# Cross-attention stage of a one-core perceiver block: scores as three fp32r products, exponentials kept in the banks of the scores

## The reference

```python
q_hk = (hidden_q @ Wq.T).reshape(Bv, Sv, H, K)            # 64 batches, 32 queries, 16 heads, K = 128
q_big = rope(jnp.einsum('bshk,hkq->bshq', q_hk, w_kc_q))
kv_r = _apply_rope(kv_c, sin_k[None], cos_k[None])         # (64, 257, 128)
q_r = jnp.einsum('bshq,hqr->bhsr', q_big, W_qr)
k_r = jnp.einsum('bld,hdr->bhlr', kv_r, W_kr)
scores = jnp.einsum('bhsr,bhlr->bhsl', q_r, k_r)
attn = jax.nn.softmax(scores, axis=-1)
ctx_c = jnp.einsum('bhsl,bld->bhsd', attn, kv_r)
ctx_lat = jnp.einsum('bhsd,hkd->bhsk', ctx_c, w_kc_kv)
return ctx_lat.transpose(0, 2, 1, 3).reshape(Bv, Sv, H * K) @ Wo.T
```

## Time and profile before

| | us |
|---|---|
| median of 3 runs | 1603.71 (1599.01 to 1604.7) |
| the profiled execution | 1602.14, its span 1600.3 |
| busy in the span | PE 1482.6, DVE 1151.1, ACT 810.9, POOL 514.5 |
| cross-attention stage | from 460 to about 960 |
| granted PE clock, mean | 0.972 |

### The profile page before, as it was taken

One profiled execution on the slowest core, in us unless ns is written; L12 is line 12 of the kernel. 1 busy time (PEld: TensorE's weight loads), 2 busy tenths in 40 slices (PEclk: granted clock), 3 DMA queues, 4 the chain that ended last, 5 costly groups with the idle time before them and its releaser, 6 DMA issues. The chain is left out here.

```text
span 1600.3 us, 26575 instructions
## 1 busy us (share of the span) xinstructions
PE 1482.6 (93%) x8136; PEld 1122.0 (70%) x8136; DVE 1151.1 (72%) x2076; ACT 810.9 (51%) x1739; POOL 514.5 (32%) x466
## 2 busy tenths in 40 slices
PE   5799999999967999999999977999898899999997
PEld 3577777777746778777787756888443478787876
DVE  6888777887649888888888753767687735656466
ACT  4566566656545555555555433555211355554554
POOL 4244333542024444444444313221351202222021
PEclk9899999999999999999999988999898899999999
DMA  4223334243575555555555514000244100000000
GB/s 153 70 83 107 105 110 125 73 123 90 187 210 117 114 120 111 131 108 125 112 121 115 127 20 172 0 0 0 84 175 159 43 1 1 27 1 26 0 27 27
DMA packets 140918, 140.06 MB, mean 88 GB/s; under 512 B 84150, under 2 KB 111926, under 8 KB 139708
## 3 DMA queue, kind: packets, MB, share of 16 engines
q1 hardware_dynamic: 140284, 138.54, 32.5%
q10 hardware_dynamic: 576, 0.81, 0.2%
HBM read 109.88 MB, written 27.39 MB: 86 GB/s over the span
## 5 line engine op out<-in xcount | busy, mean ns | idle before, releaser
L1002 ACT ACTIVATE c_e<-c_sc_ps,c_peak 128x257 f32<-128x257 f32 x256 | 119.6, 472 | 215.3 <-DVE c_peak L895 215.3
L874 POOL TENSOR_TENSOR c_mixed_low<-c_whole,c_mixed_high 128x512 fp32r<-128x512 f32 x64 | 81.6, 1275 | 256.8 <-ACT c_mixed_high L1022 256.8
L77 DVE TENSOR_TENSOR b_rot_parts_low<-b_rot,b_rot_parts_high 128x1536 fp32r<-128x1536 f32 x64 | 136.5, 2132 | 21.9 <-ACT b_rot_parts_high L541 21.9
L1578 PE MATMUL f_ps<-f_right,f_left 128*128 128x512 f32 x256 | 115.5, 613 | 8.7 <-ACT f_raw L1621 6.3
L278 POOL TENSOR_TENSOR b_turned_raw<-b_turn_part 128x384 f32<-128x384 f32 x32 | 70.0, 2189 | 164.4 <-DVE b_key_parts_low L77 163.2
L895 DVE TENSOR_REDUCE c_peak<-c_sc_ps 128x2 f32<-128x514 f32 x128 | 88.5, 691 | 44.9 <-PE c_sc_ps L1068 43.4
L70 PE MATMUL c_out_ps<-c_shared_high,c_mixed_high 128*128 128x512 f32 x256 | 112.4, 439 | 8.5 <-issue 8.5
L324 DVE TENSOR_TENSOR b_rot<-b_w_qr,b_angle 128x1536 f32<-128x1536 f32 x64 | 118.6, 1852 | 0.2
L70 PE MATMUL b_ps<-c_shared_high,b_wq_parts_high 128*128 128x512 f32 x256 | 108.4, 423 | 6.5 <-DVE c_shared_low L77 6.5
L70 PE MATMUL e_mm_ps<-folded_high,e_h_t_high 128*128 128x512 f32 x256 | 106.4, 416 | 5.7 <-DVE e_h_t_low L77 5.6
L541 ACT ACTIVATE b_rot_parts_high<-b_rot 128x1536 fp32r<-128x1536 f32 x64 | 95.2, 1488 | 24.5 <-PE b_ps L72 17.0
(11 more groups left out here) (232 smaller groups left out, 3937.2 us busy)
## 6 DMA issues: line engine op xcount, KB each, us to landing
c_ends_spread<-end_weights SPq DMA_DIRECT2D x64, 256.0 KB, 3.8
carried_queries<-x SPq DMA_DIRECT2D x7, 2048.0 KB, 11.3
b_early<-early SPq DMA_DIRECT2D x15, 640.0 KB, 4.0
f_left<-ent_in SPq DMA_DIRECT2D x16, 512.0 KB, 5.2
f_right<-ent_out SPq DMA_DIRECT2D x16, 512.0 KB, 6.5
c_q_first<-carried_queries SPq DMA_DIRECT2D x32, 224.0 KB, 3.3
c_q<-carried_queries SPq DMA_DIRECT2D x32, 224.0 KB, 3.4
b_late<-late SPq DMA_DIRECT2D x16, 320.0 KB, 3.8
```

The lines of the kernel that those rows point to most:

```text
L77: return nc.vector.tensor_tensor(low, value, high.bitcast(F32), ALU.subtract)
L874: nc.gpsimd.tensor_tensor(mixed[1][:, w, :, u], whole[:, u % 2].rearrange("p (h s) -> p h s", h=H), mixed[0][:, w, :, u].bitcast(F32), ALU ...
L1002: last = nc.scalar.activation(e[:, v, c], sc_ps[:, 2 * v + c, 0:L], ACT.Exp, bias=peak[:, v, c:c + 1], accum_out=total[:, v, c:c + 1])
L1578: return nc.tensor.matmul(ps[:, m], left[:, slot, m * P:(m + 1) * P], right[:, slot], start=k == 0, stop=k == CF - 1)
```

## The change

The queries and the rotated keys are split into high and low parts (`round_queries`, `round_keys` on ACT, `split_queries`, `split_keys` on POOL), and the scores become three fp32r products each, over 258 columns with one column of zeros. The exponentials are written over the scores in PSUM. One DVE instruction takes them from there, times the inverse sums, into `e` of 2x256; the 257th is taken by a product of its own from PSUM. So the banks are free only when both have read them. To make room, raw keys have two buffers instead of four, the rotation works in `spare`, and so the load of the next stage's weights waits for the last rotation. The last two heads of batches 0 and 1 come by DMA out of `staged`. The diff, cut:

```diff
@@ query_path, SP, last
             crossing.output_weights(sp, w_vo_dram, 2)
+            sp.wait_ge(qc_stored, 8 * HPAIRS)
+            crossing.staged_queries(sp, staged)
@@ query_path, ACT
-                    if isinstance(U, int) and U >= 2 * HPAIRS - 2:
-                        at = (H - 2 + ab) * S + base
-                        nc.scalar.activation(crossing.q[:, :, at:at + G], ...)
@@ Crossing
+    def staged_queries(self, sp, staged):
+        for u in range(2):
+            sp.dma_start(self.q[:, u, (H - 2) * S:].bitcast(F32), staged[:, u].rearrange("p h s -> p (h s)")).then_inc(self.q_loaded[u], 16)
@@ cross_attention, SP
                     if known(i, 1):
                         store_ends(i - 1, u)
-                        wait(sp, rotated_, b - BT + 1)
-                        crossing.load(sp, b, u)
+                    wait(sp, rotated_, b - 1)
+                    crossing.load(sp, b, u % 2)
+                    if known(i, 1):
                         spread_ends(i - 1, u)
-            for u in range(2, BT):
-                crossing.load(sp, u, u)
             in_tiles(sp, tile)
+            sp.wait_ge(rotated_, B)
             holo.load(sp, holo_loaded)
@@ cross_attention, POOL
+            def split_queries(b, u):
+                pool.wait_ge(q_rounded, b + 1)
+                nc.gpsimd.tensor_tensor(q[u], q[u].bitcast(F32), q_high[:, u % 2].bitcast(F32), ALU.subtract).then_inc(q_split, 1)
+            def split_keys(b, u):
+                pool.wait_ge(key_rounded, b + 1)
+                nc.gpsimd.tensor_tensor(keys[1][:, u % 2], kv_even[u], keys[0][:, u % 2].bitcast(F32), ALU.subtract).then_inc(key_split, 1)
             def tile(i, w):
                 for j in range(STEPS):
+                    if half == 0 and not (isinstance(b, int) and (b == 0 or b + 1 >= B)):
+                        split_keys(b + 1, (u + 1) % BT)
                     if half == 0 and not (isinstance(b, int) and b + 2 >= B):
                         rotate(b + 2, (u + 2) % BT, i + (u + 2) // BT)
+                    if half == 1 and not (isinstance(b, int) and b + 2 >= B):
+                        split_queries(b + 2, (u + 2) % BT)
                     if half == 1 and (u or known(i, 1)):
                         split_mixed(b - 1, (u - 1) % BT, w if u else 1 - w)
@@ cross_attention, DVE
-                for c in range(2):
-                    last = nc.vector.tensor_scalar(e[:, v, c], e[:, v, c], inverse[:, v, c:c + 1], None, ALU.mult)
-                last.then_inc(normed, 1)
+                wait(dve, turned, n - 1)
+                nc.vector.tensor_tensor(e[:, v], sc_ps[:, 2 * v:2 * v + 2, 0:END], inverse[:, v].unsqueeze(2).to_broadcast([P, 2, END]),
+                                        ALU.mult).then_inc(normed, 1)
-                dve.wait_ge(normed, n + 1)
-                nc.vector.tensor_copy(ends[:, v, 2 * half:2 * half + 2], e[:, half, :, END]).then_inc(ended, 1)
+                nc.vector.tensor_tensor(ends[:, v, 2 * half:2 * half + 2], sc_ps[:, 2 * half:2 * half + 2, END], inverse[:, half],
+                                        ALU.mult).then_inc(ended, 1)
-            parts = [two pieces of the angles, in crossing.q and q_later]
+            parts = [three pieces, in raw_pair, swapped_pair and table]
@@ cross_attention, ACT
             def exponential(n, v):
                 act.wait_ge(peaked, n + 1)
-                wait(act, turned, n - 1)
-                wait(act, ended, n - 1)
-                    last = nc.scalar.activation(e[:, v, c], sc_ps[:, 2 * v + c, 0:L], ACT.Exp, ...)
+                    last = nc.scalar.activation(sc_ps[:, 2 * v + c, 0:L], sc_ps[:, 2 * v + c, 0:L], ACT.Exp, ...)
+                    if not (isinstance(b, int) and b + 2 >= B):
+                        if half == 0:
+                            round_queries(b + 2, (u + 2) % BT, i + (u + 2) // BT)
+                        else:
+                            round_keys(b + 2, (u + 2) % BT)
@@ cross_attention, PE
                 if half == 0:
-                    pe.wait_ge(q_loaded[u], queries_in(u, t))
-                    pe.wait_ge(rotated_, b + 1)
-                wait(pe, exped, n - 1)
+                    pe.wait_ge(q_split, b + 1)
+                    pe.wait_ge(key_split, b + 1)
+                wait(pe, normed, n - 1)
+                wait(pe, ended, n - 1)
-                    last = nc.tensor.matmul(sc_ps[:, 2 * half + c, 0:L], q[u][:, at], kv_t[u], start=True, stop=True)
+                    last = multiply_parts(nc, sc_ps[:, 2 * half + c, 0:LE], [q_high[:, u % 2, at], q[u][:, at]], [a[:, u % 2] for a in keys], True, True)
```

More of the change, by code:

```diff
@@ L730, in rotate_first @@
         nc.gpsimd.tensor_tensor(part[:, 1], self.swapped[0], self.table[:, 1], ALU.mult).then_inc(self.pool_chained, 1)
+        nc.gpsimd.memset(self.keys[:, L:], 0.0).then_inc(self.padded, 1)
         pool.wait_ge(self.pool_chained, 2)
-        nc.gpsimd.tensor_tensor(self.keys[:], part[:, 0], part[:, 1], ALU.add).then_inc(self.rotated, 1)
+        pool.wait_ge(self.padded, 1)
+        nc.gpsimd.tensor_tensor(self.keys[:, 0:L], part[:, 0], part[:, 1], ALU.add).then_inc(self.rotated, 1)
     def first(self, sp):
@@ L752, in cross_attention @@
         END = L - 1
-        raw_later, swapped_later = sb("c_raw_later", [P, BT - 2, L]), sb("c_swapped_later", [P, BT - 2, L])
-        crossing.raw += [raw_later[:, u] for u in range(BT - 2)]
-        crossing.swapped += [swapped_later[:, u] for u in range(BT - 2)]
         table, raw, swapped = crossing.table, crossing.raw, crossing.swapped
         table_loaded, raw_loaded = crossing.table_loaded, crossing.raw_loaded
-        part = sb("c_part", [P, 2, L])
-        kv_later = sb("c_kv_t", [P, BT - 1, L])
-        kv_t = [crossing.keys[:]] + [kv_later[:, u] for u in range(BT - 1)]
+        part = spare[:, 0:2 * L].rearrange("p (n l) -> p n l", n=2)
+        LE = L + 1
+        kv_later = sb("c_kv_t", [P, BT - 1, LE])
+        kv_even = [crossing.keys[:]] + [kv_later[:, u] for u in range(BT - 1)]
+        kv_t = [a[:, 0:L] for a in kv_even]
         kv = pair("c_kv", [P, BT, 2, P])
-        q_later = sb("c_q", [P, BT - 2, H * S])
+        q_later = sb("c_q", [P, BT - 2, H * S], F32R)
         q = [crossing.q[:, u] for u in range(2)] + [q_later[:, u] for u in range(BT - 2)]
+        q_high = sb("c_q_high", [P, 2, H * S], F32R)
+        keys = pair("c_key", [P, 2, LE])
         peak = sb("c_peak", [P, 2, 2])
@@ L798, in queries_in @@
         def queries_in(u, t):
-            return 32 * t + (16 if u < 2 else 32)
+            return 32 * (t + 1)
         def in_tiles(engine, tile):
@@ L1016, in round_kv, with round_queries, round_keys @@
                 nc.scalar.activation(kv[0][:, u], kv_ps[:, 0:2 * P].rearrange("p (k x) -> p k x", k=2), ACT.Copy).then_inc(kv_rounded, 1)
+            def round_queries(b, u, t):
+                act.wait_ge(q_loaded[u], queries_in(u, t))
+                wait(act, scored, 2 * b - 2)
+                nc.scalar.activation(q_high[:, u % 2], q[u].bitcast(F32), ACT.Copy).then_inc(q_rounded, 1)
+            def round_keys(b, u):
+                act.wait_ge(rotated_, b + 1)
+                wait(act, scored, 2 * b - 2)
+                nc.scalar.activation(keys[0][:, u % 2], kv_even[u], ACT.Copy).then_inc(key_rounded, 1)
             def round_mixed(b, u, t, w):
```

59 lines of the change are left out of this document (36 added, 23 removed).

## The result

The changed kernel takes 1605.93 us in the median, the kernel before 1601.47 in the same session (20 runs each): ratio 1.0024, 95% interval 1.0014 to 1.0034. The forecast was -1.4 us. The time moved by about +3.8 (0.0024 of 1601.47), less than the 0.5% that I had called no change but clear of zero, and to the other side. It lies inside the forecast range of 1588 to 1617. The profiled execution has a span of 1604.1 (before 1600.3).

A forecast was written before the change was run, and what follows sets the result against it. TensorE's matmuls and the score-to-transposes chain were taken to bound a batch together (4.41 + 2.77 = 7.18 us). Terms -3.9 - 3.1 - 2.0 + 1.0 + 6.2 + 0.4 = -1.4 took 1603.7 to 1602, range 1588 to 1617.

The forecast's parts named there:

- Start: Cross-attention stage's head: first scores 5.7 us later, about five won back by the end of tile 0, net +1.0.
- tiles 3 to 13: Eleven loop tiles: batch 7.18 to 7.14 us plus no more blocking, 0.35 per tile, -3.9 us in all.
- tiles 2 and 14: Tile 14, written out, comes down from 30.30 to 28.75 us and tile 2 likewise, together -3.1.
- tile 1 and the rest of 15: Tile 1 and the part of tile 15 before its stall get shorter, -2.0 us.
- angles and what follows: Angle reduction works in three pieces instead of two, four instructions more at 0.1, +0.4 us.
- The end: Tile 15: next-stage loads wait for the last rotation, delaying batch 60's end weights and addition, +6.2 us.
- the blocking: VectorE's SBUF-only instructions held up by GpSimd; its end saves about 0.2 us per loop tile, 1.2 per written-out tile.
- the products: Six fp32r score products replace two fp32: TensorE gains 0.22 us per batch, mostly turned to waiting; 0.16 per tile left.
- tile 2 I take alike: Tile 2, the first with all its matmuls, assumed to shorten like tile 14 (30.30 to 28.75 us).
- Rival 1: Score chain itself shortens as exponentials end 0.1 us sooner in their own bank: -6.4, time 1593 to 1596; chance 0.24.
- Rivals 2 and 3: Bank reads and writes take turns in exponentials, +26, 1628, chance 0.12; GpSimd becomes the bound, +13, 1615, chance 0.14.
- Rival 4: Last tile's end stalls no longer than today: up to -6.2 us, time 1596; chance 0.06.

The follow-up runs named there:

- e3_after_start_order: Changed kernel with the last heads' staged queries loaded ahead of the third group of output weights, which moves behind the barrier; ratio 1.0007 to the kernel before.
- e1_after_end_order: Changed kernel with batch 60's end-weight store and spread issued ahead of the rotation wait and next-stage loads; 1595.08 us, ratio 0.9965 to the kernel before.
- e5_after_exp_in_sbuf: Changed kernel with exponentials, normalising and end-weight copy put back to SBUF; 1630.15 us, ratio 1.0191 to the kernel before.
- e8_after_reorder: Changed kernel, in steps scoring the next batch's first half: turned weights' parts made before the next exponentials and normalising; 1595.38 us, ratio 0.9969 to the kernel before.
- e11_all_warm_early: e6_all_three plus earlier rounding on ScalarE, first queries' low part on VectorE and 7 unused products before the first scores; ratio 0.9892 to the kernel before.
- e12_both_halves: e11_all_warm_early with the new order of turned weights before exponentials and normalising in the other steps too; ratio 0.9943 to the kernel before.
- e6_all_three: Changed kernel with the moves of e1_after_end_order, e3_after_start_order and e8_after_reorder together; 1583.51 us, ratio 0.9892 to the kernel before.
- e13_all_early: e11_all_warm_early without the 7 unused products before the first scores; ratio 0.9883 to the kernel before.
- e4_before_exp_in_banks: Kernel before with only exponentials written over the scores in their banks, normalising and end weights taken from there; ratio 0.9983 to the kernel before.

## Why the prediction was wrong

**The step that failed** is "Start": "by the end of tile 0 about five of it are won back. Net +1.0". Tile 0 gave back 0.2, so the net is +5.7. The delay itself was forecast at 5.7 and is 5.9 at the first maximum. Two errors are shown.

First, there was less to win. I took a batch of tile 0 at 7.2 before, from places where VectorE is blocked, and at GpSimd's 6.1 after. The whole tile had 27.06, 6.8 per batch, and the changed kernel needs 6.36 in tile 0's later steps (two of 3.18): 1.6 to win, not 5. e3_after_start_order, with the clock up for the mixing, shows 1.9 (25.16). From tile 1's fifth step on the output products fill TensorE.

Second, what was there to win was eaten by the clock, which no term of the prediction looked at. The fourth step of tile 0 took 4.86 where 3.18 is what it takes at the full clock, and the fourth step of tile 1 was 1.3 longer in the same way. With both at the full clock, tiles 0 and 1 would have given back some 3.7 instead of 0.7 (estimate: 0.7 + 1.7 + 1.3).

The delay alone, on the kernel before, costs 4.0, in full: tiles 0 and 1 of that kernel are as long behind a late start as behind an early one (27.08 and 29.31 against 27.06 and 29.34).

Term by term, forecast and measured: tiles 3 to 13 -3.9 and -4.5; tiles 2 and 14 -3.1 and -2.1; tile 1 and the rest of 15 -2.0 and -1.8; start +1.0 and +5.7; end +6.2 and +6.1; angles and what follows +0.4 and +0.4. With +5.7 in place of +1.0 my own sum gives +3.3; the trace has +3.7.

**The end** was forecast by its mechanism: ten us of stall (9.89), 6.2 more than before (measured 6.05). Two terms in it were off and nearly cancel, which is luck: the five loads took 2.3 us of issue (912.02 to 914.29), not 3.6, and from the store to the addition it was 8.7, not 7.9. The whole of tile 15 lost 4.7, since its other steps gained 1.3. Alone on the kernel before the wait costs 3.7.

**The loop** came out as worked out: 28.68 against 28.7, -4.5 against -3.9, with GpSimd busy 72% (5.2 per batch, forecast 5.3) and no scores waiting for it. But of the 0.35 per tile half came from a term that is not there: the blocking was worth nothing in the old loop (loop tile 29.23 with it gone), and the products gave more than the 0.16 that I gave them. That these two errors cancel is luck. The second comes from reading one batch: it has a wait of 0.15, and I took it for every batch. Over 600 to 900 us the kernel before waits 0.07 per batch (3.1 us, 12 times) and the changed one 0.19 (8.1 us, 29 times), where I had 0.15 and 0.33.

**Tiles 2 and 14** gave 0.6 and 1.5, together 2.1 instead of 3.1. The step "tile 2 I take alike" is the one that was 1.0 off.

**The rivals.** Rival 1's premise was half there: an exponential takes 444 ns into its bank, 472 before. By the Trainium skill (ScalarE: Activation LUTs, step-by-step) ScalarE reaches PSUM faster than SBUF; the two rows agree, by 28 ns. But the pair up to the reciprocal takes 1.05 as before (815.82 to 816.87, with its READ_ACCUMULATOR between), so next to nothing of it reached the chain. Rivals 2 and 3 did not happen. Rival 4 did not either: the stall came in full.

**Sum of parts on the kernel before**: start +4.0, end +3.7, exponentials -2.7, together +5.0; the whole change is +3.8. That would leave about -1 for the fp32r scores with their keys and queries and the 1.9 that they add to the start. But the four intervals together leave an uncertainty of some 3.5 us, and the parts do not simply add (fp32r scores without the banks: +1.9%), so the times do not even show its sign.

**Not settled**: what keeps TensorE's clock at half in these tiles. The length of the start does not decide it alone. e1_after_end_order, with the changed kernel's start, repeats both long steps (4.77 and 4.56); e5_after_exp_in_sbuf and e8_after_reorder, with the same start, have 3.47 and 3.48 in tile 0's fourth step and a step at a clock of 0.63 and 0.70 later; e11_all_warm_early and e12_both_halves, with one start between them, have 3.33 and 4.90; e6_all_three and e13_all_early have none in tiles 0 and 1; and e4_before_exp_in_banks, with the start of the kernel before, has one in tile 0's sixth step (4.70, clock 0.64). Unused products ahead of the first scores did not remove it.

## What to carry to other kernels

Do not count on a delay at the head of a pipelined stage being won back unless the stage's first batches are shown, by their own maxima, to run slower than the bound that is left; measure the tile that is to win it back instead of taking a batch from elsewhere, and read the granted clock there. A faster engine is worth only what the chain beside it gives up: here 0.41 of 0.89 us per tile, and the rest came by changing the order of two instructions. When a change moves a load behind a wait, read the queue behind it: the order on SP was worth 9.4 us in the changed kernel (4.6 of it in the kernel before already), and the shorter tiles gave 8.6.

## What the runs showed of the hardware

- Exponentials that read and overwrite their own bank: 444 ns on 257 elements, against 472 to 473 into SBUF (the kernel before, and the changed one with SBUF); no sign that reading and writing took turns.
- VectorE's instructions on SBUF alone are held up the more the busier GpSimd is (two points, 600 to 900 us): a 2-element copy 223 ns in the mean with GpSimd 46% busy, 545 with 69%. The product that puts the same two elements there from a bank took 150 with GpSimd at 73%.
- fp32r products of 258 columns start 0.12 apart at the full clock and 0.21 apart at half.
- The granted clock stayed near the 1.2 GHz level (0.53) through 474 to 482 us, where TensorE was busy for 7.29 of 8, and fell to 0.63 once more in 504.94 to 509.51, from 1.00. Six fp32r products of 512 columns took 2.71 us at half and 1.48 at the full clock.
